# Ternary feed-forward weights turned by DMA transposes instead of TensorE

## The reference, cut to what matters

```
def bitlinear(x, w):
    rms = rsqrt(maximum(mean(w * w), 1e-5))
    w_quant = clip(round(w * rms), -1, 1) / rms
    scale = 127 / maximum(max(abs(x), axis=-1), 1e-5)
    x_quant = clip(round(x * scale), -128, 127) / scale
    return x_quant @ w_quant.T

h = gelu(bitlinear(layernorm(t), w1))      # w1: 2048 x 512
t = t + bitlinear(h, w2)                   # w2: 512 x 2048
```

## Time and profile before

| | us |
|---|---|
| median of 3 runs | 332.18 |
| lowest, highest | 331.9, 332.73 |
| the profiled execution | 332.48 |
| its span, first to last instruction | 330.7 |
| mean granted TensorE clock in it | 0.932 |

### The profile page before, as it was taken

The page is one execution under the profiler, slowest core; times in us unless marked ns, Lnnn a source line. Parts: engine busy times, 40 slices in busy tenths (PEclk is TensorE's granted clock), DMA queues, the critical chain, the costliest instruction groups (busy, mean ns, idle before and its releaser), DMA issues. The chain is left out here.

```text
span 330.7 us, 6659 instructions
## 1 busy us (share of the span) xinstructions
PE 294.7 (89%) x2230; PEld 176.0 (53%) x2230; DVE 278.5 (84%) x667; ACT 222.2 (67%) x493; POOL 142.5 (43%) x193
## 2 busy tenths in 40 slices
PE   2458666699999999999999999999999999999994
PEld 2345534646555565646564646464746565555551
DVE  0757989789899989998999899998899899989840
ACT  2286397477775877587658666866686668666662
POOL 7405347223733374337342834184327433653330
PEclk9755679659999999999999999999999999999999
DMA  4999600000001220113010401040104010101103
GB/s 127 318 389 414 182 1 2 0 0 2 4 0 50 61 85 1 50 41 103 2 50 17 128 0 51 0 146 0 50 1 146 2 49 1 50 2 48 48 3 95
DMA packets 21449, 22.44 MB, mean 68 GB/s; under 512 B 1384, under 2 KB 18792, under 8 KB 20904
## 3 DMA queue, kind: packets, MB, share of 16 engines
q1 hardware_dynamic: 19752, 20.98, 19.1%
q10 hardware_dynamic: 1664, 1.05, 1.1%
HBM read 15.73 MB, written 6.29 MB: 67 GB/s over the span
## 5 line engine op out<-in xcount | busy, mean ns | idle before, releaser
L1125 PE MATMUL ps_o<-w2T,hq 128*128 128x512 f16 x384 | 92.6, 380 | 0.0
L1102 PE MATMUL ps_h<-w1T,xq 128*128 128x512 f16 x296 | 74.6, 389 | 0.8 <-ACT xq L491 0.8
L448 POOL TENSOR_SCALAR w_room<-w_room,q 128x2048 f32<-128x2048 f32 x24 | 47.4, 1974 | 62.7 <-DVE q L822 62.7
L491 ACT ACTIVATE w_room<-ps_h,s 128x512 f32<-128x512 f32 x74 | 50.2, 688 | 15.8 <-PE ps_h L1102 13.5
L809 DVE TENSOR_REDUCE amax<-w_room 128x1 f32<-128x1024 f32 x48 | 57.1, 1207 | 1.4 <-ACT w_room L491 1.4
L1125 PEld LDWEIGHTS ps_o<-w2T,hq 128*128 128x128 f16 x384 | 35.0, 98 | 36.9 <-ACT hq L491 3.5
L491 ACT ACTIVATE hq<-ps_t 128x512 f16<-128x512 f16 x96 | 51.4, 608 | 2.4 <-PE ps_t L1115 2.4
L1102 PEld LDWEIGHTS ps_h<-w1T,xq 128*128 128x128 f16 x296 | 27.3, 99 | 32.4 <-issue 2.6
L491 ACT ACTIVATE junk_m<-front 128x192 bf16<-128x192 f32 x64 | 20.5, 327 | 25.2 <-DVE pooled L724 25.0
L782 DVE SCALAR_TENSOR_TENSOR t<-pv,sg,xt 128x512 f32<-128x512 f32 x24 | 31.9, 1328 | 2.7 <-DVE res L832 0.5
L443 POOL TENSOR_SCALAR cen<-cen,q 128x512 f32<-128x512 f32 x24 | 16.6, 691 | 35.9 <-DVE q L804 35.9
(11 more groups left out here) (126 smaller groups left out, 491.6 us busy)
## 6 DMA issues: line engine op xcount, KB each, us to landing
x_in<-in_x SPq DMA_DIRECT2D x16, 384.0 KB, 5.2
out<-w_room SPq DMA_DIRECT2D x16, 384.0 KB, 2.6
w_room<-in_L_ffn_w SPq DMA_DIRECT2D x4, 1024.0 KB, 9.3
w_raw<-in_L_ffn_w SPq DMA_DIRECT2D x4, 1024.0 KB, 12.3
x_in<-in_x ACTq DMA_DIRECT2D x2, 384.0 KB, 3.9
fc_raw<-in_L_conv_fc_w ACTq DMA_DIRECT2D x2, 128.0 KB, 4.2
taps_rev<-in_L_conv_sa_w SPq DMA_DIRECT2D x2, 0.2 KB
taps_rev<-in_L_conv_sa_w SPq DMA_DIRECT2D x2, 0.3 KB
```

The costliest lines, as they stand in the source:

```text
L448: pool.tensor_scalar(c[:, :], c[:, :], q2[tile.par][:, 0:1], MAGIC, ALU.mult, ALU.add).then_inc(g_rounded, 1)
L491: act.activation(out_ap, in_ap, func, **more).then_inc(signal, 1)
L1102: last = pe.matmul(banks[b], xq[tile.pair.par][:, tile.s, k, :], w1T[:, k, b * 512:(b + 1) * 512], start=(k == 0), stop=(k == NC - 1))
L1125: last = pe.matmul(ps_o[:, :], hq[tile.par][:, k, :], w2T[:, k, :], start=(k == 0), stop=(k == NF - 1))
```

## The change

Each weight is rounded straight to int16 in a dense buffer of its own (the conversion to int16 rounds), by the same two engines in the same quarters. VectorE clips each quarter to -1 .. 1 and writes f16 over it. SyncE turns each quarter with one DMA transpose of 128 x 2048 f16, 0.5 MB, into w1T or w2T. The TensorE transposes, the PSUM copies on ScalarE and VectorE and the tanh bias are gone. The dense copy of w1 lies in w2T's space, that of w2 in the upper half of w1_room, each unused at that time. w1T is now laid out as blocks of 128 x 128, so the moving operand of ffn_in is four runs of 128 columns, 512 columns apart. All transposes of w1 have landed before one of w2 is issued. x of pair 3 and all later DMAs stand behind the eight transposes on SyncE. The last clip of each weight stands where the first VectorE copy stood.

```diff
-        w1T = sb("w1T", [P, NC, F], f16)
+        w1T = sb("w1T", [P, NF, NC, P], f16)
...
+        def dense(k, i, dt):
+
+            if k == 0:
+                return w2T[:, 4 * i:4 * i + 4, :].rearrange("p f c -> p (f c)").bitcast(dt)
+            return w1_room[:, 2 * F + i * F // 2:2 * F + (i + 1) * F // 2].bitcast(dt)
+
+        def flat(k, i):
+
+            return w1_room[:, i * F:(i + 1) * F] if k == 0 else w2_raw[:, i, :]
...
             load_x(Pair(2))
 
+            def turn_weights(k):
+
+                for i in range(4):
+                    sp.wait_ge(w_clipped, 4 * k + i + 1)
+                    dst = (w1T[:, 4 * i:4 * i + 4, :, :].rearrange("p f c q -> p (f c) q") if k == 0
+                           else w2T[:, :, tile_cols(i)])
+                    sp.dma_start_transpose(dst, dense(k, i, f16)).then_inc(w_turned[k][i], 16)
+
+            turn_weights(0)
+            for i in range(4):
+                sp.wait_ge(w_turned[0][i], 16)
+            turn_weights(1)
+
             for c in range(4):
...
                 pool.wait_ge(w_rms_ready, k + 1)
+                wait(pool, w_clipped, 4 * k)
                 for i in (1, 3):
-                    part = quarter(k, raw, i)
-                    pool.tensor_scalar(part, part, w_rms[:, k:k + 1], MAGIC, ALU.mult, ALU.add).then_inc(w_odd_rounded, 1)
+                    pool.tensor_scalar(dense(k, i, i16), flat(k, i), w_rms[:, k:k + 1], None,
+                                       ALU.mult).then_inc(w_odd_rounded, 1)
...
             for s in range(NT):
                 copy_x(Tile(pair1, s), (s + 1) % 2)
-            act.wait_ge(masks_ready, 2)
-            copy_weights(0, (0, 2))
             gate_tokens(pair0)
-            copy_weights(0, (4, 5, 6, 7))
...
                 dve.wait_ge(w_rms_ready, k + 1)
-                for i in (0, 2):
-                    part = quarter(k, raw, i)
-                    dve.tensor_scalar(part, part, w_rms[:, k:k + 1], MAGIC, ALU.mult, ALU.add).then_inc(w_even_rounded, 1)
+                link(dve.tensor_scalar(dense(k, 0, i16), flat(k, 0), w_rms[:, k:k + 1], None, ALU.mult))
+                clip(k, 0)
+                dve.wait_ge(w_odd_rounded, 2 * k + 1)
+                clip(k, 1)
+                link(dve.tensor_scalar(dense(k, 2, i16), flat(k, 2), w_rms[:, k:k + 1], None, ALU.mult))
+                clip(k, 2)
                 link(dve.reciprocal(w_unit[:, k:k + 1], w_rms[:, k:k + 1]))
...
+            def clip(k, i):
+
+                dve.tensor_scalar(dense(k, i, f16), dense(k, i, i16), -1.0, 1.0, ALU.max,
+                                  ALU.min).then_inc(w_clipped, 1)
+
+            def clip_last(k):
+
+                dve.wait_ge(w_odd_rounded, 2 * k + 2)
+                clip(k, 3)
...
             split_stats(pair0)
-            copy_weights(0, (1,))
+            clip_last(0)
             stats1(pair1, 0, 1, 2)
             sum_conv(pair0)
-            copy_weights(0, (3,))
             token_gate(pair0)
...
             token_max(pair1, 3, 1)
-            copy_weights(1, (1,))
+            clip_last(1)
             hidden(pair1)
...
             hidden_max(Tile(pair0, 0), 0)
-            copy_weights(1, (5,))
             scale_channels(Tile(pair1, 0), 1)
...
-                                         w1T[:, k, b * 512:(b + 1) * 512], start=(k == 0), stop=(k == NC - 1))
+                                         w1T[:, 4 * b:4 * b + 4, k, :], start=(k == 0), stop=(k == NC - 1))
...
             def weights_ready(k):
-                pe.wait_ge(*copied(k, BY_VECTOR[k][-1]))
-                pe.wait_ge(*copied(k, BY_SCALAR[k][-1]))
+                for i in range(4):
+                    pe.wait_ge(w_turned[k][i], 16)
```

More of the change, by code:

```diff
@@ L6, in metaformer_kernel @@
 def metaformer_kernel(nc, x, fc1_w, fc2_w, sa_w, w1, w2, out):
-    f32, f16, bf16 = mybir.dt.float32, mybir.dt.float16, mybir.dt.bfloat16
+    f32, f16, bf16, i16 = mybir.dt.float32, mybir.dt.float16, mybir.dt.bfloat16, mybir.dt.int16
     ALU, ACT, AX = mybir.AluOpType, mybir.ActivationFunctionType, mybir.AxisListType
@@ L105, in metaformer_kernel @@
         junk_m = sb("junk_m", [P, 2, IMG], bf16)
-        sharp_bias = sb("sharp_bias", [P, 1])
         st1 = sb("st1", [P, NT, 6])
@@ L184, in metaformer_kernel @@
         w_clipped = sem("w_clipped")
+        w_turned = [[sem(f"w{k + 1}_turned{i}") for i in range(4)] for k in range(2)]
         band_placed = sem("band_placed")
@@ L191, in metaformer_kernel @@
         w_rms_ready = sem("w_rms_ready")
-        w_even_rounded = sem("w_even_rounded")
         w_odd_rounded = sem("w_odd_rounded")
-        w_turned = sem("w_turned")
-        w_copied_s = sem("w_copied_s")
-        w_copied_v = sem("w_copied_v")
         w_unit_ready = sem("w_unit_ready")
@@ L269, in metaformer_kernel @@
         SQUARES_BY_VECTOR = [(2,), (2, 3)]
[L270 to L277, removed]
         def wait(eng, semaphore, value):
@@ L574, in squares @@
                     copy(dst, quarter(k, raw, i), squares_done, ACT.Square, accum_out=w_sq[:, k, i:i + 1])
[L576 to L581, removed]
             pair0, pair1, pair2 = Pair(0), Pair(1), Pair(2)
@@ L611, in _ @@
             gelu(Tile(pair0, 0), None, h_start, (2, 3))
-            copy_weights(1, (0,))
             token_mean(pair1, 3, 1)
-            copy_weights(1, (2, 3))
             gate_channels(pair1)
-            copy_weights(1, (4,))
             copy_xq(Tile(pair0, 1), 0)
             copy_caT(pair1)
-            copy_weights(1, (6, 7))
             sum_channels(Tile(pair1, 0))
@@ L900, in _ @@
             dve.memset(inv_n[:, :], 1.0 / (F * C)).then_inc(masks_ready, 1)
-            dve.memset(sharp_bias[:, :], -16.0 * F16_ZERO).then_inc(masks_ready, 1)
             pair0, pair1, pair2 = Pair(0), Pair(1), Pair(2)
@@ L1143, in weight_mean @@
                 pe.matmul(ms_ps[:, k:k + 1], inv_n[:, :], w_sum[:, k:k + 1], start=True, stop=True).then_inc(ms_ready, 1)
[L1145 to L1157, removed]
             def turn_fc():
@@ L1208, in _ @@
             b = turn_x(Tile(pair1, 2), 1, b)
-            turn_weights(0, w1_raw, (0, 1))
             pe.wait_ge(band_ready, 2)
             conv(pair0)
-            turn_weights(0, w1_raw, (2, 3, 4, 5, 6, 7))
             weights_ready(0)
@@ L1223, in _ @@
             ffn_in(Tile(pair0, 0), h_start, (3,))
-            turn_weights(1, w2_raw, (0, 1, 2))
             fc1(pair1)
-            turn_weights(1, w2_raw, (3,))
             fc2(pair1)
-            turn_weights(1, w2_raw, (4,))
             a = turn_xq(Tile(pair0, 1), 0, a)
-            turn_weights(1, w2_raw, (5,))
             turn_ca(pair1)
-            turn_weights(1, w2_raw, (6,))
             b = spread_ca(Tile(pair1, 0), 1, b)
             a = spread_ca(Tile(pair1, 1), 0, a)
-            turn_weights(1, w2_raw, (7,))
             ffn_in(Tile(pair0, 1), h_start, (0,))
```

## The result

| | before | after |
|---|---|---|
| median of 4 runs, us | 332.46 | 349.92 |
| lowest, highest | 331.9, 333.12 | 349.45, 349.98 |
| ratio after to before | | 1.0525, interval 1.0506 to 1.0544 |
| profiled execution; its span | 332.48; 330.7 | 349.45; 347.7 |

The changed kernel is slower by 17.5 us. Slower was forecast, but by 4.9. First the head of the page and the stretches of the kernel after, to be held against the earlier trace rows.

The account below looks back on a forecast made before the run. VectorE's order of work was taken to pay for weight preparation, with TensorE full from 70 us. First weight +4.0 and second +0.9 made +4.9, so 332.2 + 4.9 = 337.1 us, range 330.5 to 342.0.

Parts of the forecast that it names:

- GpSimd's rounding: Preparation of both weights: each GpSimd rounding of a quarter keeps its earlier 1.85 us, with no bounds given.
- Turns between the two engines: Weight preparation: VectorE and GpSimd alternate, so w1's last clip ends at 38.9 and VectorE is free for token_max at 47.3.
- The clip: VectorE's int16 to f16 clip of a quarter: 0.69 us taken, with 0.64 and 2.28 kept as bounds.
- Rival 2: Expensive end: transposes of 4.5 us each, 343.1 us, chance 0.10; or clips 1.6 us more each, 347.7 us, 0.05.
- The transposes: w1's four DMA transposes, 3.0 us each from ring free at 35.5, land at 48.9; token_max +4.0 us instead of +1.8.
- rival 1: Transposes as fast as plain loads, decided at 2.4 us each: +1.8 + 0.9 = +2.7, 334.9 us, chance 0.23.
- The second weight: w2's first rounding to the t operation takes 9.3 us against 6.57, +2.7; after savings +0.9 us.
- The three savings: After w2's preparation: split_gate to scale_channels -0.85, fc2's earlier start -0.45, a spread_ca wait absorbed -0.5 us.
- Costed at nothing: w2's transposes, pair 3's load, ScalarE's lost copies, ffn_in's four runs of 128 columns and the clock add no time.
- The clock: With 64 transposes fewer before tile 1's ffn_in, TensorE may stay longer at 1.2 GHz: none taken, 1 us kept.
- The bound of before: Before the full stretch, VectorE's order of work pays for weight preparation; TensorE and ScalarE mostly have idle time there.
- Rival 3: Relief of TensorE decides: tile 1's ffn_in starts near 68 rather than 70.11, -1.5 us net, 330.7 us, chance 0.17.

Follow-up runs that it names:

- probe: The kernel before plus eight GpSimd instructions of 128 x 2048 at its end: one operation takes 5.44 us, two take 1.97.
- pool_two_ops: The changed kernel with a multiplication by 1 as second operation in GpSimd's rounding: 335.65 us, ratio 1.0117 to the kernel before.
- ring_free: The changed kernel with GpSimd's rounding in two operations and pair 2's x load moved behind w1's transposes: 336.09 us, ratio 1.0113.
- w2_only: The kernel before with only w2 done the new way, GpSimd rounding with two operations: 333.05 us, ratio 1.0042.
- w2_only_dve: The kernel before with only w2 done the new way and VectorE rounding all of w2: 332.18 us, ratio 1.0001.
- before_act: The kernel before with ScalarE in GpSimd's place rounding quarters 1 and 3 of both weights: 333.06 us, ratio 1.0028.
- pool_i16: The kernel before with GpSimd's rounding writing int16 into the low halves, still with two operations: 334.32 us, ratio 1.0073.

## Why the prediction was wrong, step by step

- **The regime.** Right: a delay of the prologue moves the end one for one. It was 16.8 us at the first group of matmuls shown above and 17.0 at the last.
- **GpSimd's rounding, the step that failed.** It was carried over at 1.85 us each, in the sentence that VectorE's first rounding ends at 31.92 and GpSimd's second "goes first, to 33.76", and again as "1.85 (GpSimd)" twice in the second weight. The form of this instruction had changed, and it was given no bounds, though the clips, new too, had them. It takes 5.44 us alone (probe) and 5.4 to 6.5 in the kernel, and holds up one VectorE instruction each time. Four instructions at 5.44 - 1.97 = 3.47 us more are 13.9 us; pool_two_ops measured 13.7 to 14.3. With this term put right the forecast would have been 337.1 + 13.9 = 351.0, against 349.92. That it comes so near is in part luck: the rest of the sum, +4.9, was +3.8 in pool_two_ops, with the first weight 1.5 us too dear and what follows it 0.4 too cheap.
- **Turns between the two engines.** Right, and it made the error count in full. In pool_two_ops a pair of clips with a turn of GpSimd before one of them takes 2.94 us; the last clip ended at 38.0, where 38.9 was forecast, and VectorE was free for token_max at 46.1, where 47.3 was. Beside the trace stands the Trainium skill (SBUF — State Buffer, Who interferes with whom): when VectorE runs in a mode that uses both port pairs, it and GpSimd exclude each other, and the one that comes second blocks for the whole instruction of the first. The trace agrees, with the 6.40 us of two clips above.
- **The clip**, 0.69 us: measured 0.69. Rival 2's slow clip fell.
- **The transposes**, 3.0 us each, ring free at 35.5, w1 turned at 48.9: in pool_two_ops an issue was some 2.4 us at the median and w1 was turned at 47.0, so token_max was +2.45 late, not +4.0. The ring was not what they waited for (ring_free). This lies nearer to rival 1, which named 2.4 us as its limit and gave +1.8; TensorE's wait for the last transpose still ended last, which rival 1 had not. The rule of the Trainium skill that the prediction quotes (Advanced Engine Details and Errata, X-Bar Transpose), as fast as regular DMAs, would be 1.3 us by the rate of the earlier trace rows; the trace does not agree.
- **The second weight**, 2.7 - 1.8 = +0.9. In pool_two_ops the stretch to t grew by 8.76 - 6.57 = 2.2. Tile 1's ffn_in came at 72.71, +2.6 in all, hence +0.15 from this weight. Behind it more was lost: the first group of matmuls shown above came 2.9 late (87.7) and the last 3.1 (317.5), and the span of the trace is 3.2 longer. By the medians the whole was +3.8, and w2_only +1.2. The three savings, 1.8 in sum, were 2.05: from the end of t to this ffn_in it took 9.41 us, against 11.46. So the size was about right, but some 0.5 us of it was lost behind tile 1, for which the sum had nothing.
- **Costed at nothing.** The strided w1T (379 ns in both), pair 3's load and w2's transposes cost nothing, as said: the traces of after and pool_two_ops have no wait of TensorE for w2's transposes, and none for x but the one of 5.6 us at the start. The clock, for which nothing was taken and 1 us was kept, cost about nothing in pool_two_ops: from the start of tile 1's ffn_in to turn_hq it took 5.83 us, against 5.80. It cost 0.5 us in w2_only_dve, as the last point shows.
- **The bound of before.** VectorE's order was named as what pays for the weights. For w1 it stays open: in before_act VectorE was freed of 2.9 us and gained nothing, but ScalarE had been given the work. It did no harm to the sum, which went by token_max and turn_v1.
- **Rival 3**, relief of TensorE gives 330.7: no. In w2_only_dve, with no turns left for w2, ffn_in of tile 1 began at 68.89, 1.2 us early, and the time was the same, 332.18. That lead was 0.7 us by the first group of matmuls shown above (84.08) and 0.3 by the last (314.1). The first half of the loss is the clock's. These are 12 matmuls of the same ffn_in, in w2_only_dve and before:

```profile
71.24 4.11 PE L1121 MATMUL ps_h<-w1T,xq 128*128 128x512 f16 x12
```

```profile
72.49 3.58 PE L1102 MATMUL ps_h<-w1T,xq 128*128 128x512 f16 x12
```

The granted clock was 0.50 until some 74 us in both and 1.00 from there on, so that of the group which began earlier more ran at 1.2 GHz. Where the rest of the lead went was not found.

## What to carry to other kernels

When an edit changes the form of an instruction (the type it writes, or how many operations it has), its old duration is no longer evidence: give it bounds like a new one, or measure it by itself, for it is cheap to do so. On GpSimd keep two operations in a tensor_scalar, if need be with a multiplication by 1, or give the work to another engine (shown for 128 x 2048 f32 values; other sizes were not run). And where GpSimd and VectorE take turns, a slow GpSimd instruction is paid in VectorE's time, even if nobody needs its result yet.

## What was not expected of the hardware

- GpSimd's tensor_scalar over 128 x 2048 f32: 5.44 us with one operation, 1.97 us with two, into f32 or int16 alike; 0.6 us more in the kernel when int16 is written at every fourth byte (pool_i16).
- VectorE's clip from int16 to f16 of 128 x 2048 takes 0.69 us (the forecast, for which no row of before stood), about a third of its 2.28 for the squares of as many f32 values.
- A DMA transpose of 0.5 MB within SBUF moves 2080 packets of some 250 bytes (8320 and 2.10 MB for four, kernel after), keeps SyncE issuing for 1.9 to 2.5 us at the median in after, pool_two_ops and ring_free, and lands 4.3 us after issue at the soonest.
